# A closing quantisation in two passes, its stores issued by two engines

## The reference

```python
w = weights[conditions]                       # (128, 64, 64)
c = einsum('bct,bcd->bdt', x, w)
h = gelu(c @ ternary(W1).T + b1)              # W1 is 2048 x 512
y = h @ ternary(W2).T + b2                    # 512 wide
scale = max(abs(y)) / 7 + 1e-8                # over the whole tensor
q = clip(round(y / scale), -7, 7) * scale
out = x + q
```

## Time and profile before

| | us |
|---|---|
| median of three runs (lowest, highest) | 1052.09 (1050.0, 1052.19) |
| span of the profiled execution | 1048.1 |
| median less that span | 3.99 |
| TensorE busy in the span | 938.5 |
| VectorE busy | 668.6 |
| ScalarE busy | 574.4 |
| from 1/qs ready to the end of the span | 65.9 |
| DMA: read from HBM, written to it | 60.89 MB, 16.78 MB |

### The profile page before, as it was taken

How to read it: one execution, slowest core, us unless ns; L and a number is a source line. 1 busy time by engine, 2 the same in 40 slices (tenths; PEclk the granted TensorE clock), 3 DMA queues, 4 the chain that set the end, 5 groups by cost and what they waited for, 6 DMA issues and landing times.

```text
span 1048.1 us, 15055 instructions
## 1 busy us (share of the span) xinstructions
PE 938.5 (90%) x5265; PEld 449.2 (43%) x5265; DVE 668.6 (64%) x1029; ACT 574.4 (55%) x721; POOL 157.7 (15%) x213
## 2 busy tenths in 40 slices
PE   0599999999999999999999999999999999999300
PEld 0355444444444444444444444444444444444100
DVE  3599766666566756576666666665666656532698
ACT  3489382827455463728273645647382827354495
POOL 4032303030211203030303011020303030000000
PEclk9899999999999999999999999999999999999755
DMA  6510120301111112102020111121210301115898
GB/s 218 200 44 4 36 56 11 81 10 40 46 44 42 48 40 50 40 25 65 10 66 23 41 45 45 40 50 40 48 42 10 80 10 40 40 40 188 297 384 333
DMA packets 40480, 77.89 MB, mean 74 GB/s; under 512 B 3840, under 2 KB 4240, under 8 KB 39952
## 3 DMA queue, kind: packets, MB, share of 16 engines
q1 hardware_dynamic: 36192, 73.47, 23.9%
q0 software_dynamic: 4096, 3.94, 1.3%
q10 hardware_dynamic: 176, 0.27, 0.1%
HBM read 60.89 MB, written 16.78 MB: 74 GB/s over the span
## 4 chain that ended last, share of the span: by engine, by line
PE 76%; issue 11%; DVE 7%; ACT 2%; POOL 2%; DMA 1%; SPq 0%; POOLq 0%; DVEq 0%; ACTq 0%
PE ps L427 38%; PE ps L439 35%; PE ps L415 2%; DVE wts L947 1%; DVE y L941 1%; PE ps L457 1%; ACT y L636 1%; POOL ws L339 1%; DVE st L697 1%; DMA yx<-in_x 1%; DVE y L937 1%; DVE y L811 0%; DVE wts L808 0%; DMA condb<-in_itok_B 0%; DVE yc L947 0%
## 5 line engine op out<-in xcount | busy, mean ns | idle before, releaser
L427 PE MATMUL ps<-yc,wts 128*128 128x512 f16 x2048 | 447.3, 379 | 0.3 <-ACT g L568 0.3
L439 PE MATMUL ps<-wts 128*128 128x512 f16 x1920 | 419.3, 379 | 0.7 <-ACT wts L592 0.7
L427 PEld LDWEIGHTS ps<-yc,wts 128*128 128x128 f16 x2048 | 199.6, 98 | 238.5 <-ACT g L568 0.8
L439 PEld LDWEIGHTS ps<-wts 128*128 128x128 f16 x1920 | 185.8, 98 | 220.4 <-ACT wts L592 0.9
L730 DVE SCALAR_TENSOR_TENSOR wts<-g,st,wts 128x512 f16<-128x512 f32 x256 | 186.4, 749 | 143.5 <-ACT wts L573 141.8
L568 ACT ACTIVATE g<-ps,b1t,st 128x512 f32<-128x512 f32 x256 | 197.9, 773 | 116.7 <-PE ps L427 106.4
L573 ACT ACTIVATE wts<-g,st 128x512 f16<-128x512 f32 x256 | 181.0, 713 | 0.0
L555 ACT ACTIVATE xs<-yx,st 128x2048 f16<-128x2048 f32 x28 | 56.1, 2002 | 144.2 <-DVE st L765 144.2
L361 POOL PARTITION_ALL_REDUCE st<-st x46 | 21.5, 468 | 669.5 <-DVE st L699 414.3
L339 POOL DMA_INDIRECT wg<-in_L_cond_weights,ids x112 | 106.6, 952 | 41.3 <-issue 28.3
L735 DVE SCALAR_TENSOR_TENSOR y<-ps,st,b2b 128x512 f32 (+1 forms) x56 | 41.9, 748 | 77.8 <-PE ps L439 77.8
(11 more groups left out here) (127 smaller groups left out, 431.9 us busy)
## 6 DMA issues: line engine op xcount, KB each, us to landing
yx<-in_x SPq DMA_DIRECT2D x56, 512.0 KB, 6.0
wts<-in_x SPq DMA_DIRECT2D x9, 1024.0 KB, 8.1
out<-wts SPq DMA_DIRECT2D x6, 1024.0 KB, 6.3
y<-in_L_ffn_W SPq DMA_DIRECT2D x8, 512.0 KB, 8.8
y<-in_L_ffn_W SPq DMA_DIRECT2D x4, 1024.0 KB, 8.0
out<-wts SPq DMA_DIRECT2D x8, 512.0 KB, 5.1
xs<-in_x SPq DMA_DIRECT2D x2, 1024.0 KB, 5.9
yc<-in_x SPq DMA_DIRECT2D x2, 1024.0 KB, 7.8
```

What stands on the lines that cost most here:

```text
L427: last = nc.tensor.matmul(psH[:, j % HB, :], T1T[:, k, j * P:(j + 1) * P], csp[:, a, k, :], start=(k == 0 and a == 0), stop=(k == KT - 1 a ...
L439: last = nc.tensor.matmul(psY[:, r % 2, :], hsp[:, a, j, r * P:(r + 1) * P], T2T[:, j, :], start=(j == 0 and a == 0), stop=(j == HT - 1 an ...
```

## The change

The rounding stays. The second and third pass go: the add takes its first operand straight from the low half of the rounded fp32 word, read as a 16-bit integer, and nothing is clipped. Block 0 is cut into four quarters, block 1 into halves, all others are whole: 20 pieces. VectorE rounds pieces 0, 1 and 3 (quarters of block 0), ScalarE all others. Blocks 12 to 15 of x are loaded into the places of blocks 0 to 3 of y, as soon as the adds of those are done. Loads 6 to 11 lie otherwise in `wts`: load 6 waits for one quarter, 7 and 8 for two, 9 for three, 10 and 11 for all; 6, 8, 9 and 11 take two transfers each. The stores of pieces 7, 9, ..., 19 (blocks 3, 5, ..., 15) are issued by ScalarE on its own queue, each after its pass four pieces later, and the last two after its last pass.

```diff
-        HALVED = (0, 1, 2)
-        PIECES = [(b, slice(m, m + 1)) for b in HALVED for m in (0, 1)] + [(b, slice(0, 2)) for b in range(len(HALVED), NB)]
-        BY_VECTOR = [1, 3, 5, 6] + list(range(8, len(PIECES), 3))
+        ALL = slice(0, 2)
+        CUT = {0: [(slice(m, m + 1), slice(n, n + 1)) for m in (0, 1) for n in (0, 1)],
+               1: [(slice(m, m + 1), ALL) for m in (0, 1)]}
+        PIECES = [(b, m, n) for b in range(NB) for m, n in CUT.get(b, [(ALL, ALL)])]
+        LAST_OF = {b: i for i, (b, _, _) in enumerate(PIECES)}
+        BY_VECTOR = (0, 1, 3)
+        BY_SCALAR = tuple(range(7, len(PIECES), 2))
+        LEAD = 4
...
-        def q_piece(n):
...
+        def q_piece(b, m, n):
+            return y_piece(b, m, n).bitcast(I16).rearrange("p m n (t w) -> p m n t w", w=2)[:, :, :, :, 0]
...
-        xtail += [parts[:, w, 0:2, :, :] for w in range(3)]
-        xtail += [parts[:, 0:2, 2, :, :], parts[:, 0:2, 3, :, :], parts[:, 2, 2:4, :, :]]
+        xtail += [parts[:, 0:2, 0, :, :], parts[:, 2, 0:2, :, :], parts[:, 0:2, 1, :, :]]
+        xtail += [parts[:, 0:2, 2, :, :], parts[:, 2, 2:4, :, :], parts[:, 0:2, 3, :, :]]
+        APART = (6, 8, 9, 11)
         XS = len(xtail)
-        APART = (9, 10)
+        xtail += [place(y[:, b, :, :].rearrange("p r t -> p (r t)")) for b in range(NB - XS)]
...
+            sp.wait_ge(quarters_used, 1)
+            load_tail(6)
             sp.wait_ge(quarters_used, 2)
-            for b in range(6, 9):
-                load_tail(b)
+            load_tail(7)
+            load_tail(8)
             sp.wait_ge(quarters_used, 3)
             load_tail(9)
             sp.wait_ge(y_summed, NB * RT)
-            for b in range(10, XS):
-                load_tail(b)
-            for n, (b, m) in enumerate(PIECES):
-                sp.wait_ge(o_made, n + 1)
-                stored = place_stored[b] if b + XS < NB else o_stored
-                for rows, source in transfers(b, m):
-                    sp.dma_start(out_v[:, rows, :].rearrange("p (m n) t -> p m n t", n=2), source).then_inc(stored, 16)
-                if b >= 1 and m.stop == 2 and b - 1 + XS < NB:
-                    sp.wait_ge(place_stored[b - 1], 32 if b - 1 in HALVED else 16)
-                    load_tail(b - 1 + XS)
...
+            load_tail(10)
+            load_tail(11)
+            stores = 0
+            for i, (b, m, n) in enumerate(PIECES):
+                sp.wait_ge(o_made, i + 1)
+                if i not in BY_SCALAR:
+                    for rows, source, cols in transfers(b, m, n):
+                        sp.dma_start(rows_of(out_v, rows, cols), source).then_inc(o_stored, 16)
+                        stores += 1
+                if i == LAST_OF[b] and b < NB - XS:
+                    load_tail(b + XS)
+            sp.wait_ge(o_stored, 16 * stores)
...
-            def whole(n):
...
+            def store(i):
+                act.wait_ge(o_made, i + 1)
+                for rows, source, cols in transfers(*PIECES[i]):
+                    act.dma_start(rows_of(out_v, rows, cols), source).then_inc(o_stored_scalar, 16)
+
+            for i, piece in enumerate(PIECES):
+                if i not in BY_VECTOR:
+                    nc.scalar.activation(y_piece(*piece), y_piece(*piece), ACT.Identity, scale=qi, bias=magp).then_inc(q_rounded, 1)
+                if i - LEAD in BY_SCALAR:
+                    store(i - LEAD)
+                    stores += len(transfers(*PIECES[i - LEAD]))
+            for i in range(len(PIECES) - LEAD, len(PIECES)):
+                if i in BY_SCALAR:
+                    store(i)
+                    stores += len(transfers(*PIECES[i]))
+            act.wait_ge(o_stored_scalar, 16 * stores)
...
-            def clipped(n):
...
+            def added(i):
+                b = PIECES[i][0]
+                if i in BY_VECTOR:
+                    dve.wait_ge(q_rounded_vector, BY_VECTOR.index(i) + 1)
+                else:
+                    dve.wait_ge(q_rounded, i + 1 - sum(v < i for v in BY_VECTOR))
+                dve.wait_ge(xt_loaded[b], 32 if b in APART else 16)
+                nc.vector.scalar_tensor_tensor(out=x_piece(*PIECES[i]), in0=q_piece(*PIECES[i]), scalar=qs, in1=x_piece(*PIECES[i]),
                                                op0=ALU.mult, op1=ALU.add).then_inc(o_made, 1)
...
+            for i in range(len(PIECES)):
+                if i == 0:
+                    rounded(0)
+                if i + 1 in BY_VECTOR:
+                    rounded(i + 1)
+                added(i)
```

More of the change, by code:

```diff
@@ L8 @@
 I32 = mybir.dt.int32
+I16 = mybir.dt.int16
 ACT = mybir.ActivationFunctionType
@@ L99, in build, with y_piece, x_piece, transfers @@
         ymax = sb("ymax", [P, NB * RT], FP32)
-        HALVED = (0, 1, 2)
-        PIECES = [(b, slice(m, m + 1)) for b in HALVED for m in (0, 1)] + [(b, slice(0, 2)) for b in range(len(HALVED), NB)]
-        BY_VECTOR = [1, 3, 5, 6] + list(range(8, len(PIECES), 3))
+        ALL = slice(0, 2)
[6 more added lines that the diff above has]
+        LEAD = 4
         def y_of(b):
             return y[:, b, :, :] if b < NY else (yx[:, :, :], psEnd[1])[b - NY]
[L111 to L115, removed]
-        def q_piece(n):
[L119 to L123, removed]
+        def y_piece(b, m, n):
+            return (y_of(b) if b < NY else psEnd[b - NY]).rearrange("p (m n) t -> p m n t", m=2)[:, m, n, :]
+        def q_piece(b, m, n):
+            return y_piece(b, m, n).bitcast(I16).rearrange("p m n (t w) -> p m n t w", w=2)[:, :, :, :, 0]
+        def x_piece(b, m, n):
+            return xtail[b][:, m, n, :]
+        def transfers(b, m, n):
+            cut = [slice(i, i + 1) for i in range(m.start, m.stop)] if b in APART else [m]
+            return [(slice(b * RT + 2 * c.start + n.start, b * RT + 2 * (c.stop - 1) + n.stop), x_piece(b, c, n), n) for c in cut]
+        def rows_of(view, rows, n):
+            return view[:, rows, :].rearrange("p (m n) t -> p m n t", n=n.stop - n.start)
         xd = yx[:, :, :]
@@ L189, in build @@
         ym, ymr, qs, qi = stat(), stat(), stat(), stat()
-        magp, magn, zero, first_gelu = stat(), stat(), stat(), stat()
+        magp, zero, first_gelu = stat(), stat(), stat()
         ps = pb("ps", [P, HB + 4, T], FP32)
@@ L235, in build @@
         ymax_part, ymax_all, q_ready = sem("ymax_part"), sem("ymax_all"), sem("q_ready")
[L236 to L240, removed]
+        xt_loaded = [sem(f"xt_loaded{b}") for b in range(NB)]
+        q_rounded_vector, q_rounded, o_made = sem("q_rounded_vector"), sem("q_rounded"), sem("o_made")
+        o_stored, o_stored_scalar = sem("o_stored"), sem("o_stored_scalar")
         block = ctx.enter_context(nc.Block())
@@ L269, in _ @@
                 load_half(n, n * HALF + DIRECT * BB)
-            def transfers(b, m):
-                cut = [slice(i, i + 1) for i in range(m.start, m.stop)] if b % XS in APART else [m]
-                return [(slice(b * RT + 2 * c.start, b * RT + 2 * c.stop), x_piece(b, c)) for c in cut]
             def load_tail(b):
-                for rows, to in transfers(b, slice(0, 2)):
-                    sp.dma_start(to, x_v[:, rows, :].rearrange("p (m n) t -> p m n t", n=2)).then_inc(xt_loaded[b % XS], 16)
+                for rows, to, n in transfers(b, ALL, ALL):
+                    sp.dma_start(to, rows_of(x_v, rows, n)).then_inc(xt_loaded[b], 16)
             sp.wait_ge(c_made, 2 * NB)
@@ L297, in _ @@
             sp.wait_ge(y_summed, NB * RT)
-            for b in range(10, XS):
-                load_tail(b)
-            for n, (b, m) in enumerate(PIECES):
-                sp.wait_ge(o_made, n + 1)
-                stored = place_stored[b] if b + XS < NB else o_stored
-                for rows, source in transfers(b, m):
-                    sp.dma_start(out_v[:, rows, :].rearrange("p (m n) t -> p m n t", n=2), source).then_inc(stored, 16)
-                if b >= 1 and m.stop == 2 and b - 1 + XS < NB:
-                    sp.wait_ge(place_stored[b - 1], 32 if b - 1 in HALVED else 16)
-                    load_tail(b - 1 + XS)
-            sp.wait_ge(o_stored, 16 * (XS + len(APART)))
-            for b in range(NB - XS):
-                sp.wait_ge(place_stored[b], 32 if b in HALVED else 16)
+            load_tail(10)
[10 more added lines that the diff above has]
+            sp.wait_ge(o_stored, 16 * stores)
         @block.gpsimd
@@ L660, in _ @@
             act.wait_ge(y_moved, 1)
-            def rounded(n):
-                piece_y = y_piece(*PIECES[n])
-                nc.scalar.activation(piece_y, piece_y, ACT.Identity, scale=qi, bias=magp).then_inc(q_rounded, 1)
-            def whole(n):
[L667 to L680, removed]
+            stores = 0
+            def store(i):
[13 more added lines that the diff above has]
+            act.wait_ge(o_stored_scalar, 16 * stores)
         @block.vector
@@ L788, in _ @@
             nc.vector.memset(zero, 0.0).then_inc(zero_made, 1)
-            nc.vector.memset(magn, -MAGIC)
```

(11 more changed lines are left out.)

## The result

The changed kernel takes 1045.45 us at the median of four runs (1044.28 to 1046.5), beside 1051.55 for the kernel before in four runs: ratio 0.9947, 95% interval [0.9935, 0.9959]. It is faster, by 6.1 us or 0.6%. The forecast of 1044.1 was 1.4 us too low.

What follows compares the result with a forecast made beforehand. VectorE bounds the closing before, DMA after: from 982, 22.7 MB at 405 GB/s takes 56.1 us, plus 0.1, 0.8 and 1.1, ends at 1040.1; plus 4.0 gives 1044.1 us. Range: 1041.1 less 0.6 up to 1048.5.

Steps and rivals of the forecast that it cites:

- What bounds: Closing after the reciprocal at 982.2: VectorE bounds it before the change, busy 57.86 of 61.1 us; DMA decides after it.
- sum of 38.2 us: VectorE's closing work: 3 x 0.45 roundings, adds 4 x 0.67, 2 x 1.20 and 14 x 2.27, done at 1020.4.
- rival C: VectorE's adds: the strided operand takes two passes, 16 x 2.3 us more, giving 1066; chance 0.02.
- D: ScalarE's queue: issues waiting for room delay its roundings; at 6 us each, 1054.3; chance 0.03.
- ScalarE stores block 3 only at about 997: Closing, ScalarE's store of block 3: out only at about 997, yet leaves no gap in DMA's work.
- SP's issues: SP's queue in the closing: 13 pieces' stores and four late loads; last load's bytes through by 1004.5.
- DMA's terms: From 982 on: 22.7 MB at 405 GB/s, 56.1 us, plus 0.1, 0.8 and 1.1, span ending at 1040.1.
- rival B: DMA in the closing: two interleaved queues work against each other; at 300 GB/s, 1062.8; chance 0.04.
- 3.99 above the span: Whole kernel: runs' median 1052.09 lies 3.99 above the profile's span; 4.0 added to 1040.1 gives 1044.1.
- slices between 986 and 1036 under 380: DMA in the closing: such slices under 380 GB/s would show the sum failing, by A or B.
- A: DMA in the closing: rate doesn't hold, 353 GB/s, 1051.5, no change; chance 0.11 with what lies between it and forecast.
- E: DMA in the closing: no added losses and rate above 410, 22.7/0.42 = 54.0 us, giving 1041.1; chance 0.10.

## Why the prediction was right

*What bounds.* Right. VectorE's clips and roundings went and DMA took its place. Giving VectorE 5 us more or 17 us more moved the closing by about 2, taking 4.19 MB from DMA moved it by 10.

*VectorE's and ScalarE's terms.* The sum of 38.2 us came out as 38.6 (983.5 to 1022.1), with 0.55 of it a wait for x. A quarter's add takes 0.75 and its rounding 0.48; from start to start that is about 0.66 and 0.40, where 0.67 and 0.45 had been worked out from longer ones. The strided operand costs nothing (2.35 us), so rival C is out, and so is D: ScalarE's issues took 0.4 to 0.9 us each. The first store went out 1.6 us behind 1/qs (985.08), as forecast (983.7 from 982.2).

*The store four pieces behind.* My step "ScalarE stores block 3 only at about 997" was wrong. It went out at 994.39, as the add ended (994.36), though ScalarE was still at the pass that ended at 994.5 and had two more to do ahead of that store in its program. The issue doesn't wait for the passes ahead of it, so the lead costs the stores nothing. It had no effect on the sum.

*SP's issues.* I counted them at nothing, and it is right by cover alone: they took up to 9.8 us, the load of block 15 was held for 7.0 and landed 25.3 us after its issue began, not by 1004.5 as I had worked out but at 1019.7, 0.55 us after VectorE wanted it. My estimate took one queue with 405 for itself; from 994 on, ScalarE's queue takes half (2.04 MB each from 1000 to 1010).

*DMA's terms.* Counted from 1/qs, the closing is 1.4 us longer than forecast (59.3 for 57.9). The rate was 408 and not 405, which gives back 0.4. There were 22.9 MB to move and not 22.6 (22.7 less 0.2 us at 381), because less of loads 10 and 11 had moved by then: 0.6 more. The loss beside the full rate was put at 0.9, spread over the mixed stretch; it is 3.5 x (408 - 265)/408 = 1.2 in the slow stretch and 0.4 in 984 to 988: 0.7 more. The drain costs 0.9 (363, then 94) and the time behind the last byte is 0.8, together 1.7 where 1.1 had been put: 0.6 more. That adds up to 1.5. I had seen that stretch in the trace of before, but used it for rival B and not in the sum, where by its own cost it belonged: it comes with the first late load in every kernel that has one.

*What lies around the span.* The step "3.99 above the span" failed. The run profiled as changed took 1044.79 with a span of 1042.8, and every profiled run since has 1.8 to 2.1. So the span of 1048.1 must be that of the fastest run of before (1050.0), not of the median one. This made the forecast 2 us too late, and hid the 1.4 above and the 1.3 of the later start in part: 1.4 + 1.3 - 2.0 = 0.7 is what the profiled run (1044.79) lies above the forecast, and the median another 0.7 above that. That the number came so near is in part luck.

*The rivals.* By the prediction's own signs the sum was in danger twice: slices between 986 and 1036 under 380 came (344 in 986 to 988, 265 in 990.5 to 994), and VectorE did wait for x, for 0.55 us. The slices cost 1.5 us of DMA's time, the larger part of the miss; the wait cost nothing, as DMA was behind anyway. A and B, which wanted a low rate throughout, are excluded by 408 GB/s over 46 us, of which the first 25 have loads and stores on two queues, and with A the 358 of the Trainium skill (DMA: Bandwidth & Descriptors, section "Where 436 GB/s comes from") as a bound for this kernel on one core. E is out too: the losses came, the rate stayed at 408, under E's 410, and two queues don't raise it.

## What to carry to other kernels

When two engines' work over the same bytes is nearly as long as the DMA's, count the bytes from the point where they can start, divide by the rate of the longest backed-up stretch, and take that as the floor before pricing any cut in compute: here 22 us of VectorE (61.1 to 38.6 behind 1/qs) bought 6.6. Behind such a floor the queue that stores are issued on and the place where late loads land were worth nothing measurable here; what pays is bytes moved out of the bounded stretch into an idle one (three quarters of a block and half of another: about 3 us on one and the same chip). Take a profile's span against its own run's time, not against the median of others.

## What the runs showed of the hardware

- ScalarE's queue issues a DMA as soon as the semaphore in front of it allows, with up to two activations ahead of it in the program not yet run (994.39, above).
- With some 4 MB under way, by the bytes issued less those moved at 994.4 (8.4 - 4.0), the next issue on SP took 7.0 us. ScalarE's own queue went on taking 1 MB in 0.4 us then.
- A strided int16 operand, two bytes of every four, costs an add of 2048 columns the same 2.35 us, from SBUF and from PSUM.
- After a long backlog the drain can be uneven, and it differs by run: 1 us in one, 4 us in another (408, 274, 150, 117, 33 GB/s in successive microseconds). The sixteen parts of the last store then end up to 3.7 us apart; in the kernel before it was 0.2.
- Soon after the first load behind the first stores is issued, DMA runs slowly for 3 to 5 us, in all kernels that have one (265 GB/s in the changed kernel's 990.5 to 994); its share stays at 0.83 to 0.98 meanwhile. The cause is open.
